# Mixture-of-experts layer on one core: three experts' results transposed later in the next expert's unit, and their two output tiles made in reverse order

## The reference

```python
logits = xt @ gate_w
probs_full = jax.nn.softmax(logits, axis=-1)
top_p, top_i = lax.top_k(probs_full, K)
...
for k in range(K):
    e = top_i[:, k]; w = top_p[:, k]
    ...
    buf = jnp.zeros((E, cap, D), x.dtype).at[e, pos_c].set(xt * keep[:, None], mode='drop')
    h = gelu(jnp.einsum('ecd,edf->ecf', buf, w1) + b1[:, None, :])
    y = jnp.einsum('ecf,efd->ecd', h, w2) + b2[:, None, :]
    a = jnp.einsum('ecr,erd->ecd', gelu(jnp.einsum('ecd,edr->ecr', buf, wd)), wu)
    y = y + a
    tok = y[e, jnp.minimum(pos_c, cap - 1)]
    out = out + tok * keep[:, None] * w[:, None]
sh = gelu(xt @ sw1 + sb1) @ sw2 + sb2 + gelu(xt @ swd) @ swu
out = out + 0.2 * sh
```

## Time and profile before

| | |
|---|---|
| median of the runs | 182.17 us |
| profiled execution, whole | 182.13 us |
| its span, first to last instruction | 180.4 us |
| granted TensorE clock | 1.00 |
| instructions | 4053 |
| HBM read, written | 26.31 MB, 5.24 MB |
| bytes moved by DMA | 31.84 MB, mean 177 GB/s |

### The profile page before, as it was taken

One profiled execution on the slowest core, in us unless ns is written; L12 is line 12 of the kernel. 1 busy time (PEld: TensorE's weight loads), 2 busy tenths in 40 slices (PEclk: granted clock), 3 DMA queues, 4 the chain that ended last, 5 costly groups with the idle time before them and its releaser, 6 DMA issues.

```text
span 180.4 us, 4053 instructions
## 1 busy us (share of the span) xinstructions
PE 174.4 (97%) x1412; PEld 169.9 (94%) x1412; DVE 148.1 (82%) x324; ACT 145.5 (81%) x322; POOL 99.8 (55%) x109
## 2 busy tenths in 40 slices
PE   5799999999999999999999999999999999999994
PEld 6796789999999999999999999999999999999993
DVE  5658899999996986779889699799899889889821
ACT  3359889804797997897899799899799899898920
POOL 5802448320548764087977858958946655164700
PEclk9999999999999999999999999999999999999999
DMA  4494000769838493685788868868768778766232
GB/s 136 142 335 153 4 0 2 239 162 323 288 77 271 132 316 75 237 240 81 246 272 130 277 190 152 239 210 177 217 226 180 224 226 142 245 212 99 29 69 87
DMA packets 25742, 31.84 MB, mean 177 GB/s; under 512 B 4557, under 2 KB 22249, under 8 KB 25721
## 3 DMA queue, kind: packets, MB, share of 16 engines
q1 hardware_dynamic: 21720, 26.28, 45.9%
q0 software_dynamic: 3904, 5.25, 16.6%
q10 hardware_dynamic: 96, 0.04, 0.1%
HBM read 26.31 MB, written 5.24 MB: 175 GB/s over the span
## 4 chain that ended last, share of the span: by engine, by line
PE 77%; DVE 16%; DMA 3%; issue 2%; ACT 1%; ACTq 0%; DVEq 0%
PE y_ps L1027 11%; PE y_ps L1029 11%; PE y_ps L1028 11%; PE hid_ps L1027 8%; PE hid_ps L1029 8%; PE hid_ps L1028 8%; PE turn_ps L1027 4%; PE turn_ps L1029 4%; PE turn_ps L1028 4%; PE turn_ps L1191 3%; DMA cond_g<-in_L_cond_weights,itok_col 2%; DVE hid_l L721 1%; DVE at_place L824 1%; DVE key_values L846 1%; PE hid_ps L1049 1%
## 5 line engine op out<-in xcount | busy, mean ns | idle before, releaser
L721 DVE TENSOR_TENSOR hid_l<-gelu_f,hid_h 128x320 fp32r<-128x320 f32 (+2 forms) x88 | 43.3, 506 | 12.8 <-ACT hid_h L617 12.1
L468 POOL DMA_INDIRECT out_rows<-y_row,slot_tok x23 | 38.3, 1667 | 27.1 <-DVE y_row L919 12.2
L454 POOL DMA_INDIRECT slot_in<-slot_rows,slot_src x23 | 32.4, 1408 | 17.2 <-DVE slot_src L879 7.2
L1027 PE MATMUL y_ps<-w_h,hid_h 128*128 128x256 f32 x128 | 36.3, 284 | 0.1
L1028 PE MATMUL y_ps<-w_l,hid_h 128*128 128x256 f32 x128 | 36.2, 283 | 0.0
L1029 PE MATMUL y_ps<-w_h,hid_l 128*128 128x256 f32 x128 | 36.2, 283 | 0.0
L1027 PE MATMUL hid_ps<-xs_h,w_h 128*128 128x256 f32 (+2 forms) x96 | 27.9, 290 | 0.0
L616 ACT ACTIVATE gelu_f<-hid_ps,bias_s 128x320 f32<-128x320 f32 x48 | 26.4, 550 | 1.5 <-PE hid_ps L1029 1.5
L1029 PE MATMUL hid_ps<-xs_h,w_l 128*128 128x256 f32 (+2 forms) x96 | 27.5, 287 | 0.0
L1028 PE MATMUL hid_ps<-xs_l,w_h 128*128 128x256 f32 (+2 forms) x96 | 27.5, 287 | 0.0
L617 ACT ACTIVATE hid_h<-hid_ps,bias_s 128x320 fp32r<-128x320 f32 x48 | 26.6, 554 | 0.0
(11 more groups left out here) (237 smaller groups left out, 448.6 us busy)
## 6 DMA issues: line engine op xcount, KB each, us to landing
w_raw<-in_L_ffn_w SPq DMA_DIRECT2D x16, 1024.0 KB, 5.3
w_raw<-in_L_ffn_sw SPq DMA_DIRECT2D x3, 1024.0 KB, 5.4
x_in<-in_x SPq DMA_DIRECT2D x2, 512.0 KB, 4.0
w_raw<-in_L_ffn_sw SPq DMA_DIRECT2D x2, 512.0 KB, 5.9
slot_rows<-token_row SPq DMA_DIRECT2D x2, 512.0 KB, 3.3
wu_raw<-in_L_ffn_wu SPq DMA_DIRECT2D x24, 32.0 KB
out_rows<-base SPq DMA_DIRECT2D x1, 512.0 KB
slot_in<-slot_rows,slot_src POOLq DMA_INDIRECT x23
```

The costliest lines, as they stand in the source:

```text
L454: pool.indirect_dma_start(out=slot_in[par][0:n, s, :], out_offset=None, in_=x_rows, in_offset=bass.IndirectOffsetOnAxis(ap=slot_src[0:n, e ...
L468: pool.indirect_dma_start(out=out, out_offset=bass.IndirectOffsetOnAxis(ap=slot_tok[0:n, e, s:s + 1].bitcast(U32), axis=0), in_=y_row[0:n, ...
L721: dve.tensor_tensor(hid_l[:, j - 1, 0:n], gelu_f[:, j % 3, 0:n], hid_h[:, j - 1, 0:n].bitcast(F32), ALU.subtract).then_inc(hid_split, 1)
L1027: pe.matmul(out_ap, l_h, r_h, start=start, stop=False)
```

## The change

1. `turn_results` of experts 0, 1 and 2 moves in PE's queue from behind hidden tile 2 of the next unit to behind `turn_slots` of that unit, so that it stands after all nine hidden tiles, beside the transposes of the gathered rows. That of expert 3 stays behind tile 2 of unit 4.
2. `weigh_rows` of experts 0, 1 and 2 moves on DVE from behind split 3 to behind split 8. That of expert 3 stays.
3. `expert_out` makes tile m = 1 first and m = 0 second. ACT copies them, and PE turns them, in that order. The wait for DVE's weighing goes to tile m = 0 and asks for the first weighed tile; `turn_results` waits for both copies before its first transpose.

```diff
+        OUT_ORDER = range(KD - 1, -1, -1)
...
-                for m in range(KD if e < ROWS_FROM else 0):
-                    act.wait_ge(y_made, y_before(e + 2) + (m + 1))
+                for i, m in enumerate(OUT_ORDER if e < ROWS_FROM else []):
+                    act.wait_ge(y_made, y_before(e + 2) + (i + 1))
                     act.activation(y_t[:, m, :], y_ps[m][:, 0:SLOTS], ACT.Copy).then_inc(y_copied, 1)
...
-                    if rows and j == 3:
+                    if rows and j == (3 if e >= ROWS_FROM else HT - 1):
                         if e - 1 < ROWS_FROM:
                             weigh_rows(e - 1, 1 - par)
...
             def expert_out(e, m, par, size):
-                if m == 0:
+                first = m == OUT_ORDER[0]
+                if first:
                     pe.wait_ge(w2_lo, v * CHUNKS + CHUNKS)
                     pe.wait_ge(wu_lo, v + 1)
                     if e == 0:
                         pe.wait_ge(base_done, EARLY)
-                    else:
-                        pe.wait_ge(y_weighted, e * ST)
+                if e > 0 and m == 0:
+                    pe.wait_ge(y_weighted, (e - 1) * ST + 1)
...
                 for f in range(NF):
-                    if m == 0:
+                    if first:
                         pe.wait_ge(hid_split, hid_count(e + 2, f + 1))
...
             def turn_results(e):
-                pe.wait_ge(y_copied, e * KD + 1)
                 if e > 0:
                     pe.wait_ge(y_weighted, e * ST)
-                for m in range(KD):
-                    if m > 0:
-                        pe.wait_ge(y_copied, e * KD + (m + 1))
+                for m in OUT_ORDER:
+                    pe.wait_ge(y_copied, e * KD + KD)
...
-                        if m == KD - 1:
+                        if m == OUT_ORDER[-1]:
                             ins.then_inc(y_turned, 1)
...
                     for j in range(HT):
                         hidden(e + 2, j, other, e + 1, xs_h, xs_l, slice(0, size), size)
-                        if 0 < e <= ROWS_FROM and j == TURNED_AT:
+                        if e == ROWS_FROM and j == TURNED_AT:
                             turn_results(e - 1)
                     if e < E - 1:
                         turn_slots(e + 1, other, (sizes[e + 1] + P - 1) // P)
+                    if 0 < e < ROWS_FROM:
+                        turn_results(e - 1)
                     if e < ROWS_FROM:
-                        for m in range(KD):
+                        for m in OUT_ORDER:
                             expert_out(e, m, other, size)
```

## The result

| | before | changed |
|---|---|---|
| median of the runs beside each other | 182.08 us (181.72 to 182.44, 6 runs) | 184.3 us (184.01 to 185.42, 6 runs) |
| profiled execution, its span | 182.13 us, 180.4 us | 185.42 us, 183.7 us |

The changed kernel is slower: its time is 1.0134 of the time before, with an interval of 1.0117 to 1.0151. That lies outside the range of 181.8 to 182.8 us. The two profiled executions differ by 3.3 us, the medians by 2.2 us.

The account below looks back on a forecast made before the run. The prediction took PE's gapless queue to bound the kernel. All six parts summed to 0, so it forecast 182.2 us against a median of 182.17, with a range of 181.8 to 182.8 us.

Parts of the forecast that it names:

- What bounds the kernel: PE works off its queue without a gap; a unit is as long as its matmuls times their 0.13 us pitch.
- the alternative that I drew from it: Only the matmuls' own cost, or a wait that makes PE's full queue stand still, can change the time.
- PE, the transposes: Six transposes of L1207 moved in units 1 to 3, two blocks made one: 0.0 us, bound 0.28 us gained.
- the two rivals on the block: Merged transposes save a slot per border, 181.8 us, chance 0.08; or clock halves in blocks of twelve, 186.1 us, chance 0.01.
- PE, the output tiles: 25 matmuls into y_ps[1] before 25 into y_ps[0], wait moved to the second tile with 0.7 us cover: cost 0.
- ACT and DVE: ACT gains 0.46 us; DVE's 1.17 us of weighings move, L897 ends at 84.64 in unit 1, cover 0.50: cost 0.
- The rival that I gave most to: Start of unit 2: DVE late for PE, which waits for L897; 182.6 to 183.1 us, chance 0.14.
- The sign that was named for this rival: A PE wait for L897, L898 in the changed kernel, would prove that DVE becomes late for PE.
- The chance of 0.15 for slower: Whole kernel: 0.14 for DVE late for PE plus 0.01 for the clock falling in the block of twelve.
- SP: Loads of w1 issued 0.7 us later behind DVE's wd and wu parts; cover shrinks from 2.8 to 1.6 us: cost 0.
- POOL and its queue: Unit 1's scatter starts about 81.4, 4.4 us later; following casts and scatters stay covered or catch up: cost 0.
- the term in which the scatter of unit 3 lands at 117.4: Third DMA issued at 113.3 plus 4.05 us to land, before DVE weighs in unit 4 at 118.87: cover 1.5 us.

Follow-up runs that it names:

- two buffers: Changed kernel with token_row as second buffer for weighed rows, DVE waiting for the scatter of two units back: 182.32 us, ratio 1.0019.
- a place half way: Changed kernel with results turned behind hidden tile 4 and weighed behind split 5, between old and new places: 182.43 us, ratio 1.0005.

## Why the prediction was wrong

**What bounds the kernel** was right, and so was the alternative that I drew from it: the time changes by what the matmuls cost or by a wait that makes the full queue stand. It was a wait.

**PE, the transposes**: right, 0. The weight loads in the changed kernel run through twelve transposes at a pitch of 0.11 us and on:

```profile
77.17 0.71 PEld L1193 LDWEIGHTS turn_ps<-ident,slot_in 128*128 128x128 f32 x6
77.85 0.14 PEld L1207 LDWEIGHTS y_ps<-ident,y_t 128*128 128x128 f32 x1
...
78.50 0.19 PEld L1150 LDWEIGHTS y_ps<-low_s,wu_s 128*128 128x128 f32 x1
```

The block takes 1.33 us for 12 (77.17 to 78.50), no border of a block was worth a slot, and unit 1 is 15.02 us long at a clock of 1.00. So the two rivals on the block fell: the merged block saved nothing, and the clock did not fall in it. By the Trainium skill's page "TensorE: Matmul & The Clock Gate", section "Part 4: PE-mode transpose", a longer block was a risk; in this kernel the trace shows none for twelve in a row.

**PE, the output tiles**: right by itself, 0: the tile order alone cost nothing, and with two buffers, where the moved wait is in the kernel too, nothing was left to tell. The moved wait at the head of y_ps[0] is where PE stood in unit 2, but what it waited for was DVE behind the scatter.

**ACT and DVE**: right. ACT's wait of the earlier trace rows is gone. In unit 1 the low parts of the next rows begin at 83.59 and end at 84.46, where I had 84.64:

```profile
83.59 0.87 DVE L898 TENSOR_TENSOR xs_l<-turn_ps,xs_h 128x320 fp32r<-128x320 f32 x2
```

The rival that I gave most to, DVE late for PE at the start of unit 2 because of 1.17 us of moved work, did not come there: PE began unit 2 at 85.07 without a wait. DVE did become late for PE, but in units 2 and 4 and because it was itself kept waiting. The sign that was named for this rival, a wait of PE for L898, did show at the start of unit 3, for 0.3 us, and it too came from the scatter. The chance of 0.15 for slower was right in sign and had the wrong mechanism behind it.

**SP**: the cover held for w1, the only load that I had worked out. For the w2 load there was none left: ACT waited 1.64 us for it in unit 2, beside the slow scatter. No wait of PE in this kernel names ACT, so this is not shown to have cost anything:

```profile
98.07 2.19 ACT L566 ACTIVATE w_h<-w_raw 128x512 fp32r<-128x512 f32 x4 [1.64 <-DMA w_raw<-in_L_ffn_w]
```

**POOL and its queue**: this is the step that failed, the term in which the scatter of unit 3 lands at 117.4 with a cover of 1.5 us, cost 0, and unit 2 is not asked about at all. It landed at 123.06, and that of unit 1 at 96.89; DVE waited 2.77 and 2.66 us, PE behind it, and units 4 and 2 became 1.94 and 1.46 us longer. The scatter's start in unit 1 was right (81.88, I had 81.4). Two things were not.

First, "in unit 2 the tile is weighed about 94.8 ... and POOL is free about 94.5": I asked when POOL would be free for the next scatter, and not when the scatter of unit 1 would have landed, though `weigh_rows` waits for just that. The check was made for unit 4 alone.

Second, the durations. Had I made the check for unit 2 with my own terms (issues of 1.64 with gaps of 0.31, 4.05 from the third issue to its landing) it would have read 81.4 + 3.9 + 4.05 = 89.35 against 94.23, when DVE wanted y_row (96.89 less its wait of 2.66): a cover of 4.9 us. What came was 96.89. For unit 3 I had written 117.4, and it came at 123.06, 5.7 us later, in four parts: the first issue 1.6 later (111.01 for 109.4, since unit 2 had grown by 1.5), 0.2 for the second issue, 1.6 for the third (3.35 for 1.77), 2.3 for the landing (4.6 behind the issue's end for the 2.3 that lie in 4.05). The cover of 1.5 could not hold that, and would not have held without the growth of unit 2: late in unit 3 alone, the first issue came at 109.2, and DVE still waited 2.13 us.

Both terms came from rows at other places: the issue from one that met no run of low parts, the landing from the end of the program, where no weights are loaded any more. The row that would have warned me stood in the trace of the kernel before: an issue of 2.98 us in unit 1 (84.81 to 87.79), at the time to which the scatter was about to be moved. I counted the whole stretch "from scatter to cast" as 12.25 us, in which the slow gather was contained, and so moved the total but not what was inside.

Shown by runs: that the wait for the single y_row carries the loss (two buffers, with the block of twelve and the tile order still in the kernel), that DVE's low parts draw out the issues, that the loads delay the landing, and that a place half way costs nothing that can be told. Left open: why the kernel with the transposes put back is no faster than the changed one, what draws out the gather in the opening, and how the waits spread over executions that left no profile (the changed kernel's runs lie from 184.01 to 185.42 us). No version tried is faster than the kernel before: it has no gap of PE in the units that one could close.

## What to carry to other kernels

When a step is moved, follow its result to the end of its buffer's life: who may write there next, and what has to be over by then. Take the length of each moved instruction from the place to which it goes, not from where it stood: look what has been slow there so far, even if nobody waited for it. And test the cover with a place half way: here 1.4 us of delay were free, and 4.9 us cost 2.2 us in the median and 3.3 in the profiled execution.

## What the runs showed of the hardware

- **POOL's indirect DMAs were issued 1.5 to 3 times as slowly beside DVE's subtractions.** The first two issues of unit 1's scatter took 1.91 and 1.56 us with the low parts cut, and 2.94 and 3.78 us beside them; a gather's took about 1.0 us, and 2.98 us at that place in the kernel before. The Trainium skill's page "GPSIMD Engine Reference", section "8. Key points", names contention with VectorE instructions that have two inputs in SBUF, and the low parts are such; this case agrees and gives the size, but no run here shows the mechanism. Its page "SBUF — State Buffer", section "Who interferes with whom", reports a probe in which a `tensor_tensor` did not hold up a DMA issued by GpSimd, and infers that writing descriptors needs the write side only; it also says that such an instruction contends with GpSimd where GpSimd reads SBUF. Here the indirect DMAs, which take their row numbers from SBUF, were held up by `tensor_tensor`. The measurement decides that they are; whether it is by these reads was not tested.
- **A scatter that adds to HBM landed slowly beside weight loads**: in unit 1, 5.8 us after its last issue had ended in the changed kernel, about 1.8 us with those loads cut.
- **The granted clock fell after a gap of PE**: it read 1.00 before and 0.72 over the 4 us in which the gap of 3.69 us ended, although the kernel's queue was full again at once; 1.6 us were lost with it. The gaps of 0.85 and 1.75 us in the changed kernel left it at 1.00 in their units. The length of the gap does not settle it: in the opening of the same execution the clock read 0.50 behind a gap of 1.8 us, and in the kernel with one expert's loads cut a gap of 1.7 us at the same place left it at 1.00.
